# The softmax sums of the last unit shared out by alternate key tiles between GpSimd and VectorE

## The reference

```python
qkv = x @ w_qkv                                   # 128 -> 3 x 1024
sim = einsum('bhid,bhjd->bhij', q, k) / 8
attn = softmax(sim)                               # over 2048 keys
out = einsum('bhij,bhjd->bhid', attn, v)
x = x + out @ w_out + b_out
...
x = x + fp4_linear(silu(fp4_linear(ln(x), w_gate)) * fp4_linear(ln(x), w_up), w_down)
```

## Time and profile before

| | us |
|---|---|
| median of 3 runs | 1351.75 (1350.59 to 1353.01) |
| the profiled execution | 1352.66 |
| its span, first to last instruction | 1350.8 |
| busy: TensorE, GpSimd, ScalarE, VectorE | 1269.7, 1054.3, 890.6, 855.6 |
| mean granted TensorE clock | 0.976 of 2.4 GHz |

### The profile page before, as it was taken

The page is one execution under the profiler, slowest core; times in us unless marked ns, Lnnn a source line. Parts: engine busy times, 40 slices in busy tenths (PEclk is TensorE's granted clock), DMA queues, the critical chain, the costliest instruction groups (busy, mean ns, idle before and its releaser), DMA issues.

```text
span 1350.8 us, 24752 instructions
## 1 busy us (share of the span) xinstructions
PE 1269.7 (94%) x7429; PEld 667.8 (49%) x7429; DVE 855.6 (63%) x2350; ACT 890.6 (66%) x1272; POOL 1054.3 (78%) x457
## 2 busy tenths in 40 slices
PE   4999999999999999999999999999999998888566
PEld 3555555555455555555454555555555554443245
DVE  6656666656566556666566555666656667786694
ACT  4767667777676677676677667767667766654243
POOL 4488888898788888888888888888898888779142
PEclk9999999999999999999999999999999999899687
DMA  2000000000000000000000000000000000000001
GB/s 63 2 9 2 1 2 10 1 1 2 3 10 1 2 1 9 2 1 2 5 7 2 1 1 9 2 2 1 4 1 1 1 2 1 2 1 1 0 1 32
DMA packets 45951, 6.66 MB, mean 5 GB/s; under 512 B 37344, under 2 KB 45664, under 8 KB 45808
## 3 DMA queue, kind: packets, MB, share of 16 engines
q1 hardware_dynamic: 45584, 4.41, 2.6%
q0 software_dynamic: 224, 0.54, 0.1%
HBM read 3.75 MB, written 1.05 MB: 4 GB/s over the span
## 4 chain that ended last, share of the span: by engine, by line
PE 84%; DVE 7%; issue 5%; POOL 2%; ACT 1%; DMA 0%; POOLq 0%; SPq 0%; DVEq 0%; ACTq 0%
PE o_ps L1180 32%; PE s_ps L1028 24%; PE mx_ps L1050 8%; PE mx_ps L1043 4%; PE misc_ps L1170 3%; PE misc_ps L1162 2%; PE misc_ps L1015 2%; PE misc_ps L993 2%; PE s_ps L1036 1%; PE misc_ps L994 1%; PE misc_ps L995 1%; POOL acc_pool L508 1%; PE s_ps L1270 1%; DVE split L743 1%; PE misc_ps L999 1%
## 5 line engine op out<-in xcount | busy, mean ns | idle before, releaser
L508 POOL TENSOR_TENSOR acc_pool<-acc_pool,probs 128x1024 f32<-128x1024 f32 x352 | 853.3, 2424 | 49.7 <-POOL acc_pool L508 41.6
L625 ACT ACTIVATE probs<-s_ps 128x1024 f32<-128x1024 f32 x512 | 525.5, 1027 | 70.5 <-PE s_ps L1028 29.2
L797 DVE CUSTOM_DVE_ANT_0 summed<-mx_ps,rise 128x512 bf16<-128x512 f32 x503 | 344.8, 686 | 331.5 <-issue 290.6
L1180 PE MATMUL o_ps<-probs,vv 128*64 128x512 f32 x2048 | 498.6, 607 | 6.1 <-ACT probs L625 6.1
L545 ACT ACTIVATE rise<-mx_ps 128x512 f32<-128x512 f32 x503 | 300.0, 596 | 270.4 <-PE mx_ps L1043 258.5
L1180 PEld LDWEIGHTS o_ps<-probs,vv 128*64 128x64 f32 x2048 | 127.0, 136 | 223.0 <-issue 179.6
L1043 PE MATMUL mx_ps<-k_raw,q_hi 64*128 64x512 f32 x503 | 224.0, 445 | 9.1 <-DVE part_max L797 7.9
L1050 PE MATMUL mx_ps<-k_hi,q_hi 64*128 64x512 f32 x503 | 223.6, 445 | 7.4 <-issue 3.6
L1028 PE MATMUL s_ps<-q_hi,k_hi 64*128 64x512 f32 x1024 | 205.7, 395 | 0.9 <-ACT probs L625 0.8
L1028 PE MATMUL s_ps<-q_hi,k_lo 64*128 64x512 f32 x1024 | 203.9, 392 | 0.0
L1028 PE MATMUL s_ps<-q_lo,k_hi 64*128 64x512 f32 x1024 | 203.7, 391 | 0.0
(11 more groups left out here) (160 smaller groups left out, 1098.1 us busy)
## 6 DMA issues: line engine op xcount, KB each, us to landing
mrow<-neg_max SPq DMA_DIRECT2D x256, 0.5 KB, 2.0
wqkv<-in_L_attn_w_qkv SPq DMA_DIRECT2D x8, 192.0 KB, 2.8
y<-in_L_attn_x SPq DMA_DIRECT2D x4, 256.0 KB, 4.4
out<-y SPq DMA_DIRECT2D x4, 256.0 KB, 2.3
wo<-in_L_attn_w_out SPq DMA_DIRECT2D x8, 64.0 KB, 1.9
wx<-in_L_ffn_w_down POOLq DMA_DIRECT2D x1, 176.0 KB, 6.2
wx<-in_L_ffn_w_gate POOLq DMA_DIRECT2D x1, 128.0 KB, 4.5
wx<-in_L_ffn_w_up POOLq DMA_DIRECT2D x1, 128.0 KB, 5.1
```

Of the source, the lines that this page charges most:

```text
L508: pool.tensor_tensor(acc, first, probs[:, j % P_BUFS, :, :], ALU.add) \
L625: act.activation(probs[:, j % P_BUFS, :, :], s_ps[:, j % 2, :, :], ACT.Exp, scale=SCALE) \
L797: dve.tensor_tensor_reduce(summed[:, s % 2, :], mx_bank(h, pair), rise[:, h, :], 1.0, LOWEST, ALU.add, ALU.max, part_max[:, slot:slot + 1] ...
L1180: ins = pe.matmul(o_ps[DH * h:DH * (h + 1), :], vv[par(w)][:, j, DH * h:DH * (h + 1)], probs[:, j % P_BUFS, h, :], start=(j == 0), stop=(j ...
```

## The change

In the last unit only, tiles are shared out differently. GpSimd adds tiles 0, 2, 4, 6, 8, 10 and 12 (6 adds), VectorE tiles 1, 3, 5, 7, 9, 11, 13, 14 and 15 (8 adds, each at the head of its step in VectorE's list, ahead of what else the step has). The waits for free buffers follow that split. The joining add goes; TensorE waits for both sums and makes the denominators of both, in four products that accumulate in PSUM instead of two. GpSimd's scaling in the unit stands behind the add of tile 8 instead of tile 9, and the scaling behind the unit follows the last add directly. All other units keep their code.

```diff
+END_POOL = list(range(0, STEPS - 2, 2))
+END_DVE = [t for t in range(STEPS) if t not in END_POOL]
...
+        def added(tiles, t):
+
+            return max(tiles.index(t), 1)
+
+        def pool_free(it, w, j, last):
 
             t = j - P_BUFS
+            if t >= 0 and last and w == BODY - 1:
+                if t in END_POOL:
+                    return pool_adds, after(it, POOL_ADDS, w, added(END_POOL, t))
+                return dve_adds, at(it, DVE_ADDS, w, DVE_ADDS + added(END_DVE, t))
...
-                    for j in range(1, POOL_TILES):
-                        if j == 1:
+                    end = last and w == BODY - 1
+                    for k, j in enumerate(END_POOL[1:] if end else range(1, POOL_TILES)):
+                        if k == 0:
...
-                        if last and w > CHUNKS and j == 9:
+                        if last and w > CHUNKS and j == (8 if end else 9):
                             times_scale(w - CHUNKS - 1)
...
+                    if not end:
+                        pool.wait_ge(pool_adds, after(it, POOL_ADDS, w, POOL_ADDS))
+                        pool.wait_ge(dve_adds, at(it, DVE_ADDS, w, 2 * DVE_ADDS))
+                        pool.tensor_tensor(acc, acc, acc_dve[:, w % 2, :, :], ALU.add).then_inc(den_acc, 1)
...
+                        if last and w == BODY - 1 and j in END_DVE[1:]:
+
+                            k = END_DVE.index(j)
+                            dve.wait_ge(p_ready, after(it, STEPS, w, j + 1))
+                            if k > 1:
+                                dve.wait_ge(dve_adds, at(it, DVE_ADDS, w, DVE_ADDS + k - 1))
+                            dve.tensor_tensor(sums, probs[:, END_DVE[0], :, :] if k == 1 else sums, probs[:, j % P_BUFS, :, :],
+                                              ALU.add).then_inc(dve_adds, 1)
...
+                    end = w == BODY
+                    if end:
+                        pe.wait_ge(pool_adds, after(it, POOL_ADDS, w - 1, len(END_POOL) - 1))
+                        pe.wait_ge(dve_adds, at(it, DVE_ADDS, w - 1, DVE_ADDS + len(END_DVE) - 1))
+                    else:
+                        pe.wait_ge(den_acc, after(it, 1, w, 1))
                     for h in range(2):
                         ins = pe.matmul(ps[DH * h:DH * (h + 1), :], ones[:, :], acc_pool[:, (w - 1) % 2, h, :],
-                                        start=True, stop=True)
+                                        start=True, stop=not end)
+                    if end:
+                        for h in range(2):
+                            ins = pe.matmul(ps[DH * h:DH * (h + 1), :], ones[:, :], acc_dve[:, (w - 1) % 2, h, :],
+                                            start=False, stop=True)
```

More of the change, by code:

```diff
@@ L321, in par @@
             return (w // CHUNKS) % 2
-        def pool_free(it, w, j):
+        def added(tiles, t):
+            return max(tiles.index(t), 1)
+        def pool_free(it, w, j, last):
             t = j - P_BUFS
+            if t >= 0 and last and w == BODY - 1:
+                if t in END_POOL:
+                    return pool_adds, after(it, POOL_ADDS, w, added(END_POOL, t))
+                return dve_adds, at(it, DVE_ADDS, w, DVE_ADDS + added(END_DVE, t))
             if t >= 0:
@@ L499, in body @@
                     acc = acc_pool[:, w % 2, :, :]
-                    for j in range(1, POOL_TILES):
-                        if j == 1:
+                    end = last and w == BODY - 1
+                    for k, j in enumerate(END_POOL[1:] if end else range(1, POOL_TILES)):
+                        if k == 0:
                             pool.wait_ge(den_acc, after(it, 1, w, 1))
                         else:
-                            pool.wait_ge(pool_adds, after(it, POOL_ADDS, w, j - 1))
+                            pool.wait_ge(pool_adds, after(it, POOL_ADDS, w, k))
                         pool.wait_ge(p_ready, after(it, STEPS, w, j + 1))
-                        first = probs[:, 0, :, :] if j == 1 else acc
+                        first = probs[:, 0, :, :] if k == 0 else acc
                         pool.tensor_tensor(acc, first, probs[:, j % P_BUFS, :, :], ALU.add) \
                             .then_inc(pool_adds, 1)
-                        if last and w > CHUNKS and j == 9:
+                        if last and w > CHUNKS and j == (8 if end else 9):
                             times_scale(w - CHUNKS - 1)
-                    pool.wait_ge(pool_adds, after(it, POOL_ADDS, w, POOL_ADDS))
-                    pool.wait_ge(dve_adds, at(it, DVE_ADDS, w, 2 * DVE_ADDS))
-                    pool.tensor_tensor(acc, acc, acc_dve[:, w % 2, :, :], ALU.add).then_inc(den_acc, 1)
+                    if not end:
+                        pool.wait_ge(pool_adds, after(it, POOL_ADDS, w, POOL_ADDS))
+                        pool.wait_ge(dve_adds, at(it, DVE_ADDS, w, 2 * DVE_ADDS))
+                        pool.tensor_tensor(acc, acc, acc_dve[:, w % 2, :, :], ALU.add).then_inc(den_acc, 1)
                     if last and w >= CHUNKS:
@@ L623, in body @@
                         act.wait_ge(pv_done, at(it, STEPS, w, j + 1))
-                        act.wait_ge(*pool_free(it, w, j))
+                        act.wait_ge(*pool_free(it, w, j, last))
                         act.activation(probs[:, j % P_BUFS, :, :], s_ps[:, j % 2, :, :], ACT.Exp, scale=SCALE) \
@@ L931, in body @@
                                 block_scales(w - CHUNKS)
+                        if last and w == BODY - 1:
+                            continue
                         if j == POOL_TILES + 1:
@@ L1158, in misc @@
                 elif name == "den":
-                    pe.wait_ge(den_acc, after(it, 1, w, 1))
+                    end = w == BODY
[4 more added lines that the diff above has]
+                        pe.wait_ge(den_acc, after(it, 1, w, 1))
                     for h in range(2):
                         ins = pe.matmul(ps[DH * h:DH * (h + 1), :], ones[:, :], acc_pool[:, (w - 1) % 2, h, :],
-                                        start=True, stop=True)
+                                        start=True, stop=not end)
[3 more added lines that the diff above has]
+                                            start=False, stop=True)
                 else:
```

## The result

| | before | after |
|---|---|---|
| median us, 6 runs each | 1351.83 (1350.54 to 1353.01) | 1343.05 (1339.82 to 1345.15) |
| ratio, 95% interval | | 0.9934 [0.9919, 0.9948] |
| profiled execution, its span | 1352.66, 1350.8 | 1341.83, 1339.8 |

The change makes the kernel 8.9 us faster (7.0 to 10.9 by the interval). I had forecast 4.4 us and a range that ended at 1343.2: the direction was right, the size half of what came. The changed kernel's six runs spread over 5.3 us, those of before beside them over 2.5 (though 23 of them in a later series over 7.1).

What follows compares the result with a forecast made beforehand. GpSimd's adds were taken to bound the last unit; denominators ending at 1256.26 instead of 1260.59 gave 4.3 us, taken as 4.4 for a possible fast clock: 1352.66 to 1348.3 us profiled, median 1347.3; range 1343.2 to 1351.2, forecast's own 1345.5 to 1348.9.

Steps and rivals of the forecast that it cites:

- The bound and the path: Last unit: GpSimd's adds bound it, and everything after the denominators' end at 1260.59 us hangs on that moment.
- The turns between GpSimd and VectorE: Last unit: VectorE instructions with two SBUF operands and GpSimd's take turns, a whole instruction at a time; GpSimd add 2.25-2.4 us.
- D1 to D3: VectorE's adds of tiles 1 and 3, tile 5 and tile 7, forecast to end at 1222.5, 1229.15 and 1234.9 us.
- D5: VectorE's fifth add in the last unit, forecast to end at 1243.1 us on the profiled execution's time line.
- the sum of turns is the same: Middle of the last unit: if VectorE wins the turn at 1235.8 us, its fifth add still ends at 1243.
- TensorE's wait for line 822 (now 834): Last unit: TensorE's projection waits for VectorE's multiplication from 1234.5 to 1238.7, leaving TensorE idle 4.2 us.
- The low clock that one rival feared: Last unit: the projection's wait drops TensorE's clock, 8.7 us of work taking up to 17.4; slower kernel, chance 0.08.
- D8: VectorE's last add in the last unit, of tile 15, forecast to end at 1252.2 us on the profiled time line.
- Denominators: After VectorE's last add: eight TensorE records instead of four, at the low clock, 3.96 us, ending at 1256.26.
- Everything behind, unchanged and shifted as a whole: From the denominators to the span's end: length unchanged at 90.2 us, only starting earlier.
- a small chance of the fast price: Denominators' records at TensorE's full clock, 1.8 us more gain; it raised the forecast gain from 4.3 to 4.4 us.
- The rival without turns: Last unit: large adds on VectorE and GpSimd take no turns or far fewer; gain 11 or 7.5 us, chance 0.15.

Runs made afterwards that it cites:

- E3: The changed kernel without GpSimd's six adds in the last unit, so the even tiles are missing from the sum; ratio to before 0.9914 [0.9899, 0.9928].
- E6: The changed kernel with the last unit's projection two steps later in TensorE's list, behind the scores of tiles 13 and 14; ratio to before 0.9948 [0.9935, 0.9961].
- E1: The kernel before with seven extra TensorE products, results unused, ahead of the last unit's denominators; ratio to before 0.9982 [0.9973, 0.9991].
- E12: The changed kernel once more, with the same code; ratio to before 0.9937 [0.9918, 0.9956].
- E11: The kernel before with seven extra products ahead of the denominators and seven ahead of product pair 2 of the feed-forward block; ratio to before 0.9965 [0.9951, 0.9979].
- E5: The kernel before with only the last unit's joining add dropped, denominators made from both sums in four products; ratio to before 0.9974 [0.9964, 0.9983].

## Why the prediction was wrong in size

By its own steps, counted from the common event (forecast less 1.65 us to stand on the time line after):

- *The bound and the path*: right. The unit was GpSimd's, and everything behind the denominators hangs on them.
- *The turns between GpSimd and VectorE*: right, to 0.3 us, though not for two-operand instructions alone. D1 to D3, line 834 and D5 were forecast to end at 1220.85, 1227.5, 1233.25, 1237.0 and 1241.45; they ended at 1220.9, 1227.35, 1232.93, 1236.69 and 1241.32. E3 shows that these turns, with ScalarE's waits for GpSimd, cost 3.9 us. E6 shows that the layout was luckier than I argued: "the sum of turns is the same" holds at one place, not where GpSimd's add isn't ready yet, and there a turn is worth 2.2 us.
- *TensorE's wait for line 822 (now 834)*: right, 3.63 us against 4.2. The low clock that one rival feared followed (granted 0.64 from 1236.84 to 1241.40), but VectorE's last add came no later than forecast, so it was off the path, as E6 also says.
- *D8*: forecast 1250.55, measured 1250.07, half a microsecond early.
- *Denominators*: **the term that failed.** "I take the slow price", 3.96 us; the eight records took 1.94. The gap was forecast at 3 us and measured 2.18, and I read 1.66 us behind 1.79 us of idleness as proof that the low clock follows. That row only shows that it can. Both profiles of the changed kernel have this gap; one paid 1.98 up to the first reciprocal, the other 3.23.
- *Everything behind, unchanged and shifted as a whole*: **the assumption that failed with it.** I put the stretch behind the denominators at no change. It gave 1.25 us in proj (E1: 1.24 with nothing else changed) and 1.3 in the tail. The first comes with the shorter idle stretch ahead of the denominators: proj is 6.3 us in all with a gap under 4 us and 7.5 or more in the three with a longer one. The second doesn't: E1 has the tail of before (82.67), and so has E12 (82.63), while E6, with a den of 3.45, has 81.36. It is the clock in the tail's own idle stretches, and whether it comes varies between executions. One of my signs of being wrong was that the last 90 us change by over 1.5: from the denominators to the end it was 90.2 us before and 87.6 after. I had given the clock as a reason for a loss in three rivals, and for a gain only as "a small chance of the fast price", worth 0.1 us in the sum.
- *The rival without turns* had a chance of 0.15 for gains of 6.5 us or more, and the 8.9 us of the runs lie there. Its mechanism is refuted all the same: the second add took 3.40 us, and D8 ended 5.6 us behind its 1244.45 (1246.1 less 1.65).

Summed: 4.3 forecast, + 0.5 for the adds, + 2.0, + 1.25, + 1.3 for the clock = 9.35, the profile's difference. E11 makes up 3.7 us of before's path (4.7 by the runs) out of idle time alone, so that the clock can give this much stands on its own experiment; its 1.6 us in the tail come from the extra products there and lie only partly where the changed kernel's 1.3 do. In an execution like E12's it is 4.3 + 0.5 + 0.75 (den 3.23 against my 3.96) + 1.24 (proj) = 6.8.

That by the profile; how often a run of the changed kernel has the short den and the short tail isn't shown, so its median of 8.9 us can't be cut into the same terms.

Not settled: why the runs of E5 are faster than its profile allows, and what decides between the two clocks at a gap of 2.2 us. The changed kernel with extra products in that gap, the counterpart of E1, was not run. A version with GpSimd adds in the last unit forced into VectorE's favourable turn was not tried.

## What to carry to other kernels

When a change shortens a stretch in which TensorE idles, price the idleness as well: what follows can run at the other clock, and the difference was as large here, in the first profile, as the work saved. Where a gap has been seen with either clock behind it, treat it as a coin and give the range both sides, upward too. Where GpSimd and VectorE work on SBUF side by side, write out their turns as a schedule; here it predicted to 0.3 us, until in E6 one operand came 0.76 us later and a whole turn changed hands.

## What the hardware showed that I had not expected

- The same program, with the same idle time of 2.17 us, ran its next eight records in 1.94 us in one execution and 3.19 us in another, and its untouched last part in 81.33 and 82.63.
- Seven useless products of 4.31 us in an idle stretch shortened the rest by 1.6 to 3.1 us in the profiles; the stretch right behind them gained 2.0 to 2.4.
- With a slower start of a unit (E6) VectorE finished 2.2 us sooner, as GpSimd missed its turn.
- The turn of a loop of identical code took 40.93 us in one profile and 38.49 in the next, measured between two GpSimd joins; the granted clock just behind it was 0.67 in the first and 1.00 in the second.
